# An LSTM layer on one core: the input projections of the first sixteen steps laid out anew, and the weight pieces for later steps formed in halves

## The reference

```python
xW = jnp.einsum('ntd,dk->tnk', x, Wx) + b

def step(carry, xw_t):
    prev_h, prev_c = carry
    a = xw_t + prev_h @ Wh
    i = jax.nn.sigmoid(a[:, :Hdim])
    f = jax.nn.sigmoid(a[:, Hdim:2 * Hdim])
    o = jax.nn.sigmoid(a[:, 2 * Hdim:3 * Hdim])
    g = jnp.tanh(a[:, 3 * Hdim:])
    next_c = f * prev_c + i * g
    next_h = o * jnp.tanh(next_c)
    return ((next_h, next_c), next_h)
_, hs = jax.lax.scan(step, (h0, c0), xW)
x = x + jnp.transpose(hs, (1, 0, 2))
```

## Time and profile before

| | us |
|---|---|
| median of 3 runs | 2538.99 |
| lowest to highest | 2538.72 to 2539.34 |
| the profiled execution, its own time | 2539.07 |
| its span, first to last instruction | 2537.3 |
| TensorE matmuls busy | 2518.5 (99%) |
| VectorE busy | 1983.7 (78%) |
| ScalarE busy | 1237.1 (49%) |
| mean granted TensorE clock | 0.999 |

### The profile page before, as it was taken

How to read it: one execution, slowest core, us unless ns; L and a number is a source line. 1 busy time by engine, 2 the same in 40 slices (tenths; PEclk the granted TensorE clock), 3 DMA queues, 4 the chain that set the end, 5 groups by cost and what they waited for, 6 DMA issues and landing times.

```text
span 2537.3 us, 157236 instructions
## 1 busy us (share of the span) xinstructions
PE 2518.5 (99%) x67166; PEld 1795.3 (71%) x67166; DVE 1983.7 (78%) x8532; ACT 1237.1 (49%) x5216; POOL 0.2 (0%) x4
## 2 busy tenths in 40 slices
PE   8999999999999999999999999999999999999998
PEld 3577777777777777777777777777777777777776
DVE  7877777777777777777777777777777777777776
ACT  5444444444444444444444444444444444444444
POOL 0000000000000000000000000000000000000000
PEclk9999999999999999999999999999999999999999
DMA  4101101011011010110110101101101011011000
GB/s 169 36 17 33 30 20 33 19 31 33 17 33 29 21 33 18 32 33 17 33 28 22 33 17 33 33 17 33 26 24 33 17 33 33 17 33 25 24 17 18
DMA packets 141017, 76.01 MB, mean 30 GB/s; under 512 B 8492, under 2 KB 139708, under 8 KB 140220
## 3 DMA queue, kind: packets, MB, share of 16 engines
q1 hardware_dynamic: 140548, 75.40, 11.3%
q10 hardware_dynamic: 440, 0.20, 0.0%
HBM read 42.02 MB, written 33.55 MB: 30 GB/s over the span
## 4 chain that ended last, share of the span: by engine, by line
PE 98%; DVE 1%; DMA 0%; ACT 0%; SPq 0%; issue 0%; DVEq 0%
PE odd L281 26%; PE even L287 25%; PE odd L287 25%; PE even L281 13%; PE s1t_sum L281 6%; PE plain_even L287 1%; PE plain_odd L287 1%; PE plain_odd L300 1%; PE plain_even L300 1%; DMA w_raw<-in_L_cond_Wx_dram 0%; DVE xw_lo L792 0%; DVE hw_lo L792 0%; DVE hT_hi L620 0%; DVE w_raw L789 0%; DVE f_c L671 0%
## 5 line engine op out<-in xcount | busy, mean ns | idle before, releaser
L671 DVE TENSOR_TENSOR f_c<-i_f,c_state 128x64 f32<-128x64 f32 x992 | 225.2, 227 | 438.0 <-ACT i_f L521 438.0
L521 ACT ACTIVATE i_f<-odd 128x128 f32<-128x128 f32 x496 | 142.9, 295 | 529.3 <-PE odd L287 529.3
L281 PE MATMUL odd<-xw_lo,xT_hi 128*32 128x256 f16 x7936 | 388.6, 273 | 0.0
L281 PE MATMUL odd<-xw_hi,xT_hi 128*32 128x256 f16 x7936 | 388.6, 273 | 0.0
L281 PE MATMUL odd<-xw_hi,xT_lo 128*32 128x256 f16 x7936 | 388.6, 273 | 0.0
L287 PE MATMUL odd<-hw_hi,hT_hi 128*32 128x512 f16 x3968 | 385.9, 379 | 1.2 <-DVE hT_hi L620 1.2
L287 PE MATMUL even<-hw_hi,hT_hi 128*32 128x512 f16 x3968 | 385.9, 379 | 0.3 <-DVE hT_hi L620 0.3
L287 PE MATMUL odd<-hw_lo,hT_hi 128*32 128x512 f16 x3968 | 385.9, 379 | 0.0
L287 PE MATMUL even<-hw_lo,hT_hi 128*32 128x512 f16 x3968 | 385.9, 379 | 0.0
L521 ACT ACTIVATE i_f<-even 128x128 f32<-128x128 f32 x496 | 142.9, 295 | 417.9 <-PE even L287 417.9
L537 ACT ACTIVATE tanh_c<-c_state 128x64 f32<-128x64 f32 x992 | 269.1, 271 | 97.8 <-DVE c_state L681 38.8
(11 more groups left out here) (113 smaller groups left out, 4141.4 us busy)
## 6 DMA issues: line engine op xcount, KB each, us to landing
x_ring<-in_x_dram SPq DMA_DIRECT2D x252, 128.0 KB, 2.8
out_dram<-x_ring SPq DMA_DIRECT2D x252, 128.0 KB
w_raw<-in_L_cond_Wx_dram SPq DMA_DIRECT2D x3, 1024.0 KB, 9.8
w_raw<-in_L_cond_Wh_dram SPq DMA_DIRECT2D x3, 1024.0 KB, 15.4
w_raw<-in_L_cond_Wx_dram SPq DMA_DIRECT2D x2, 512.0 KB, 4.8
w_raw<-in_L_cond_Wh_dram SPq DMA_DIRECT2D x2, 512.0 KB, 18.9
x_ring<-in_x_dram SPq DMA_DIRECT2D x6, 64.0 KB, 17.7
out_dram<-x_ring SPq DMA_DIRECT2D x5, 64.0 KB
```

The lines of the kernel that those rows point to most:

```text
L281: mm = nc.tensor.matmul(bank[j * N:(j + 1) * N, cols], x_part[:, pair, n, k * N:(k + 1) * N], w_part[:, n, k, j, :], start=False, stop=Fal ...
L521: nc.scalar.activation(i_f_half, bank_half, ACT.Sigmoid, scale=UNSCALE).then_inc(if_ready[two], 1)
L671: nc.vector.tensor_tensor(half_of(f_c[:, :], two), half_of(i_f[:, P:2 * P], two), half_of(c_state[:, :], two), ALU.mult)
```

## The change

The four banks `plain_even`, `plain_odd`, `even[1]` and `odd[1]` now serve the plain steps in turn. While the input weight tiles arrive, TensorE adds, after step 0's products of a tile, the hi x hi and hi x lo products of steps 1 to 3 of that tile, in place of `keep_going`; biases for steps 2 and 3 are spread after the first tile, and the lo x hi products follow for step 1 after the last input tile and for steps 2 and 3 after step 0. The 144 passes of steps 4 to 15 are dealt out over steps 1 to 13 by `passes_done`. `plain_recur` takes both products of hT_hi before that of hT_lo. Inputs of steps 1 to 3 are cast and split after the first tile. FORMED pieces are formed and split by halves of 128 x 512 with new steps for each half, casts and the bias difference have new steps, and ScalarE's seed of a pair's bank in steps 13 and 15 waits for o_gate. The `keep_going` bursts after the recurrent tiles stay.

```diff
-FORM_AT = (0, 1, 2, 3, 4, 5, 6, 6)
-CAST_AT = (3, 4, 5, 6, 7, 8, 9, 10)
-REST_AT = (7, 8, 9, 10, 11, 12, 13, 14)
-BIAS_AT = 7
+FORM_AT = ((1, 1), (2, 2), (3, 3), (4, 4), (5, 5), (6, 6), (7, 8), (8, 9))
+CAST_AT = (8, 9, 4, 5, 6, 7, 10, 11)
+REST_AT = ((12, 12), (13, 13), (6, 7), (9, 10), (10, 10), (11, 11), (14, 14), (14, 15))
+BIAS_AT = 0
+
+AHEAD = 4
+
+PASSES = 12
+
+
+def passes_done(step):
+
+    return min(34 * step // 3, PASSES * (PLAIN - AHEAD)) if step < 13 else PASSES * (PLAIN - AHEAD)
...
+        plain_banks = (plain_even, plain_odd, even[1], odd[1])
...
-            def plain(t):
-                if t == 1:
-                    pe.wait_ge(bias_ready, 1)
-                else:
-                    pe.wait_ge(plain_seeded, t - 1)
+            def spread_bias(*steps):
+
+                for t in steps:
+                    for j in range(J):
+                        mm = nc.tensor.matmul(plain_bank(t)[j * N:(j + 1) * N, :], spread[:, j * N:(j + 1) * N],
+                                              bias_rows[:, :], start=False, stop=False, skip_group_check=True)
+                return mm
+
+            def plain_hi(t, k):
+                for w in (xw_hi, xw_lo):
+                    plain_add(plain_bank(t), xp_hi, (0, 1), w, t, k)
+
+            def plain_lo(t):
                 pe.wait_ge(xp_ready, t + 1)
-                for part, w in ((xp_hi, xw_hi), (xp_hi, xw_lo), (xp_lo, xw_hi)):
-                    for k in range(J):
-                        plain_add(plain_bank(t), part, (0, 1), w, t % GROUP, k)
+                for k in range(J):
+                    plain_add(plain_bank(t), xp_lo, (0, 1), xw_hi, t, k)
+
+            def plain_passes(first, last):
+
+                for n in range(first, last):
+                    t, (part, k) = AHEAD + n // PASSES, divmod(n % PASSES, J)
+                    if n % PASSES == 0 or n == first:
+                        pe.wait_ge(plain_seeded, t + 1 - AHEAD)
+                        pe.wait_ge(xp_ready, t + 1)
+                    x_part, w_part = ((xp_hi, xw_hi), (xp_hi, xw_lo), (xp_lo, xw_hi))[part]
+                    plain_add(plain_bank(t), x_part, (0, 1), w_part, t % GROUP, k)
 
             def plain_recur(t):
                 pe.wait_ge(hT_hi_ready[0], t + 1)
                 if t == 1:
                     pe.wait_ge(hw_hi_ready, J * GATES)
-                for k in range(J):
-                    recur_add(plain_bank(t), hT_hi, hw_hi, k)
+                    pe.wait_ge(hw_lo_ready, J)
+                for w in (hw_hi, hw_lo):
+                    for k in range(J):
+                        recur_add(plain_bank(t), hT_hi, w, k)
                 pe.wait_ge(hT_lo_ready, t + 1)
                 for k in range(J):
-                    recur_add(plain_bank(t), hT_lo, hw_hi, k)
-                if t == 1:
-                    pe.wait_ge(hw_lo_ready, J)
-                for k in range(J):
-                    mm = recur_add(plain_bank(t), hT_hi, hw_lo, k)
+                    mm = recur_add(plain_bank(t), hT_lo, hw_hi, k)
                 mm.then_inc(gates_ready, 1)
...
-                    keep_going()
+                    if k == 0:
+                        spread_bias(2, 3)
+                        pe.wait_ge(bias_ready, 1)
+                        pe.wait_ge(xp_hi_ready, AHEAD)
+                    for t in range(1, AHEAD):
+                        plain_hi(t, k)
+                plain_lo(1)
                 pe.wait_ge(hT_lo_ready, 1)
...
-                if plain_steps > 1:
-                    plain(t + 1)
+                if plain_steps == PLAIN:
+                    for ahead in range(2, AHEAD):
+                        plain_lo(ahead)
+                elif plain_steps > 0:
+                    plain_passes(passes_done(t - 1), passes_done(t))
...
+            spread_bias(0, 1).then_inc(bias_spread, 1)
             for t in range(PLAIN):
                 step(t, t % BODY, BODY, t // BODY, PLAIN - t)
             pe.wait_ge(xw_lo_ready[P_A22], 2)
...
+                    else:
+                        act.wait_ge(o_ready, t + 1)
                     seed(r % 2)
...
-                if plain_steps > 2:
+                if plain_steps > AHEAD:
                     act.wait_ge(o_ready, t + 1)
-                    seed_plain(t + 2)
+                    seed_plain(t + AHEAD)
...
-                        act.wait_ge(w_diff_ready, piece + 1)
+                        act.wait_ge(w_diff_ready, 2 * piece + 2)
                         split_x_hi(n, *W_PLACE[n], k)
...
-                    if n == W_B11 and k < 2:
-                        cast_plain(k)
+                    if n == W_B11 and k == 0:
+                        cast_plain(0)
                 if k == 0:
                     act.wait_ge(bias_spread, 1)
                     nc.scalar.activation(bias_scaled[:, :], plain_odd[:, :], ACT.Copy).then_inc(bias_ready, 1)
-                if k == 2:
-                    cast_plain(2)
-                    cast_plain(3)
+                    for t in range(1, AHEAD):
+                        cast_plain(t)
...
                 for piece, (n, k) in enumerate(FORMED):
-                    if plain_steps > 0 and FORM_AT[piece] == t:
-                        form(n, k)
-                    if plain_steps > 0 and REST_AT[piece] == t:
-                        split_x_lo(n, *W_PLACE[n], k)
+                    for g in range(2):
+                        if plain_steps > 0 and FORM_AT[piece][g] == t:
+                            form(n, k, g)
+                        if plain_steps > 0 and REST_AT[piece][g] == t:
+                            split_x_lo(n, *W_PLACE[n], k, (g,))
...
-                v.then_inc(xw_lo_ready[n], 1)
+                if halves[-1]:
+                    v.then_inc(xw_lo_ready[n], 1)
```

More of the change, by code:

```diff
@@ L289, in recur_add, with plain_bank @@
                 return mm
-            def plain_bank(s):
-                return plain_odd if s % 2 else plain_even
+            def plain_bank(t):
+                return plain_banks[t % AHEAD]
             def plain_add(bank, part, halves, w, slot, k):
@@ L335, in first_step @@
             def first_step():
-                bank = plain_even
+                bank = plain_bank(0)
                 pe.wait_ge(xp_ready, 1)
@@ L475, in seed_plain @@
             def seed_plain(t):
-                nc.scalar.activation((plain_odd if t % 2 else plain_even)[:, :], bias_scaled[:, :],
+                nc.scalar.activation(plain_banks[t % AHEAD][:, :], bias_scaled[:, :],
                                      ACT.Copy).then_inc(plain_seeded, 1)
@@ L511, in step @@
                 if plain_steps > 0:
-                    bank = plain_odd if s % 2 else plain_even
+                    bank = plain_banks[t % AHEAD]
                     nc.scalar.activation(i_f[:, :], bank[:, IF], ACT.Sigmoid, scale=UNSCALE).then_inc(if_ready[0], 1)
@@ L733, in step @@
                 if plain_steps == PLAIN:
-                    rest_plain(2)
-                    rest_plain(3)
                     transpose_x(1, 1, 0)
@@ L775, in form_bias, with form @@
                                         ALU.subtract).then_inc(bias_diff_ready, 1)
-            def form(n, k):
+            def form(n, k, g):
                 k0, gates = W_PLACE[n]
-                place = raw(k0 + k, gates)
-                a, b, op, was, formed = {P_S3: (place, raw(k, 1), ALU.subtract, W_B22, 0),
-                                         P_S1: (place, raw(k, 0), ALU.subtract, W_B12, k + 1),
-                                         P_S2: (raw(2 + k, 1), place, ALU.add, W_B11, 2 + k + 1),
-                                         P_A22: (place, raw(k, 0), ALU.subtract, W_B21, 4 + k + 1)}[n]
+                place = raw(k0 + k, gates, g)
+                a, b, op, was, formed = {P_S3: (place, raw(k, 1, g), ALU.subtract, W_B22, 0),
+                                         P_S1: (place, raw(k, 0, g), ALU.subtract, W_B12, k + 1),
+                                         P_S2: (raw(2 + k, 1, g), place, ALU.add, W_B11, 2 + k + 1),
+                                         P_A22: (place, raw(k, 0, g), ALU.subtract, W_B21, 4 + k + 1)}[n]
                 dve.wait_ge(xw_hi_ready[was], k + 1)
@@ L787, in form @@
                 if formed:
-                    dve.wait_ge(w_diff_ready, formed)
+                    dve.wait_ge(w_diff_ready, 2 * formed)
                 nc.vector.tensor_tensor(place, a, b, op).then_inc(w_diff_ready, 1)
@@ L793, in split_lo, with split_x_lo @@
                                                       op0=ALU.mult, op1=ALU.subtract)
-            def split_x_lo(n, k0, gates, k):
+            def split_x_lo(n, k0, gates, k, halves=(0, 1)):
                 dve.wait_ge(xw_hi_ready[n], k + 1)
@@ L799, in split_x_lo @@
                 lo = xw_lo[:, n, k, :, :].rearrange("p j (g f) -> p g j f", g=2)
-                for g in range(2):
+                for g in halves:
                     v = split_lo(src[:, 2 * gates + g, :, :], hi[:, g, :, :], lo[:, g, :, :])
```

(14 more changed lines are left out.)

## The result

The changed kernel takes **2547.68 us** (median of 7 runs, 2546.13 to 2549.50) against 2538.86 for the kernel before, timed beside it (7 runs, 2538.72 to 2539.34): a ratio of 1.0033, 95% interval 1.0024 to 1.0043. It is 8.8 us slower where I forecast 1.9 slower. The profiled run took 2546.85, 7.78 more than the 2539.07 of the profiled run of before.

The account below looks back on a forecast made before the run. It took TensorE as the bound, with a 2.54 us chain limiting the changed steps; 2539.07 + 0.10 for step 16's later start + 1.70 for the clock's fall = 2540.9 us, range 2538.4 to 2542.0 for 8 in 10.

Parts of the forecast that it names:

- Steps 1 to 15: Input steps: eight of the first twelve last 5.13 us, four 5.18; their last recurrence ends 3.49 us early, at 106.70.
- The step of rows 5 and 6: From a recurrence's end to the next, a chain of 2.54 us against 2.59 of fill: removed work buys 0.05 a step.
- The stall: Before step 16, TensorE waits some 3.6 us for A22's last half on VectorE; step 16 begins 0.10 us later than before.
- The clock: Behind the stall before step 16, TensorE's clock falls to its lower level: +1.7 us (0 to 1.8), chance 0.50.
- Rival 1: Before step 16 the stall is there but the clock holds: 2539.2 us, chance 0.41.
- Step 0 ends as now: At the start, the added early work is hidden and wins nothing: step 1's recurrence starts at 32.09 as before.
- The sum: Whole run: the profiled 2539.07 plus 0.10 for step 16's start and 1.70 for the clock gives 2540.9 us.
- Rival 2: Before step 16, the A22 wait doesn't bind; step 16 starts at 109.5: 2536.0 us, chance 0.04.
- Rival 3: In step 0, the denser start is still granted half speed and ends 7.1 us late: 2546.3 us, chance 0.03.
- Rival 4: In the input steps, all 112 matmuls that leave count, at 54 ns each: 2532.5 us, chance 0.02.

Follow-up runs that it names:

- 3: Kernel before with only the half pieces at their new steps, TensorE's order kept: 2546.01 us, ratio 1.0027.
- 9: Changed kernel with pieces formed whole, one rest placed otherwise and 27 pad matmuls, so both programs have their old lengths; A22's wait not moved: 2541.57 us.
- 1: Changed kernel with TensorE's A22 wait moved from ahead of the loop to its first use in close_odd: 2540.85 us, ratio 1.0009.
- 7: 2 with pieces formed whole again, giving VectorE's program its old length: 2538.70 us.
- 2: Changed kernel with the half pieces formed, cast and split in the steps of before: 2541.10 us.
- 12: Kernel before with 101 small matmuls (202 instructions) more on TensorE before the loop: 2542.43 us, ratio 1.0014.
- 8: 2 with 27 small matmuls more on TensorE and pieces formed whole, both programs at their old lengths: 2536.08 us, ratio 0.9988 to the kernel before.
- 10: 9 with the A22 wait moved to close_odd and 26 pad matmuls: 2536.22 us.
- 11: Kernel before with 64 one-column memsets more on VectorE at its start: 2539.89 us.
- 6: 2 with 27 small matmuls more on TensorE at its start, giving its program the old length: 2538.25 us.
- 5: Kernel before with 16 one-column memsets more at VectorE's start: 2541.30 us, ratio 1.0009.

## Why the prediction was wrong, and where it was right

**Steps 1 to 15: right.** From step 1's recurrence to the end of step 15's I gave 74.61 us (8 x 5.13, 4 x 5.18, 10.26 and 2.59); measured 107.81 - 33.17 = 74.64. The starts of the recurrences lie 5.13 us apart in eight of the first twelve steps and 5.19 in four; a step of 5.13 holds 92 matmuls of 54 ns, 4.97, so the pauses of 0.15 before hT_hi are there. The step of rows 5 and 6, a chain of 2.54 against a fill of 2.38, was the right way to see that most of the removed matmuls buy nothing. ("From step 1 TensorE has no pause" passes over the 0.51 before 37.96, which the sum itself uses.)

**The stall: right, 0.2 short.** I gave 5.99 from the end of step 15's recurrence to step 16's; it is 6.20. The last half ends at 113.67 and TensorE starts 0.34 later, not 0.05: in 3 and 9 it starts 0.34 to 0.35 behind the half as well.

**The clock: right in kind, its size in part luck.** +1.7 forecast, 1.6 measured in after's profile, and it fell in after, 3 and 9, behind pauses of 3.4 to 3.7 us. But behind the same stall the fall cost 2.7 us in the profiles of 3 and 9, above the 0 to 1.8 that I allowed. Rival 1, the clock that holds, had 0.41; for a pause of this length that was too much. Behind the shorter pause of step 508 it fell in the profiles of 1 (2.22 us) and 7 (2.57) and not in those of after, 2 and 12 (1.93 to 2.08); by their spans it fell in four of ten runs of 1 and three of ten of 7.

**"Step 0 ends as now": off by 1.08** in this profile. In it tile 0 of the recurrent weights is cast at 20.26 and not at 18.40, behind its DMA, and VectorE's sixteen splits start at 21.00 and pause 0.33, against 20.40 and no pause. ScalarE's rows, before and after:

```profile
18.40 4.52 ACT L572 ACTIVATE hw_hi<-w_raw 128x512 f16<-128x512 f32 x8 [0.83 <-DMA w_raw<-in_L_cond_Wh_dram]
```

```profile
20.26 2.19 ACT L604 ACTIVATE hw_hi<-w_raw 128x512 f16<-128x512 f32 x4 [2.08 <-DMA w_raw<-in_L_cond_Wh_dram]
```

In the profiles of the other kernels with the new start step 1's recurrence starts at 32.78 (1), 32.05 (2), 31.87 (8), 31.57 (9) and 32.65 (10), and with the old one at 31.69 (3) to 33.09 (11). So the new start doesn't make it late as such; it moves by up to 1.6 us from one profile to the next. I read one row of a DMA's arrival as fixed.

**The sum: wrong by what wasn't in it.** Adding the terms to the profiled execution's 2539.07 took over two things as unchanged that were not: the 1.77 us outside the span and the tail behind the loop. The diff takes 54 instructions from TensorE's program and gives 16 to VectorE's. I costed them by the time they run and not by where they push the code behind them. That is the failed step: **+2.6 to 2.85** for the block behind the loop (7 less 8, 2 less 6, clock falls included; in after's profile, without a fall, it is 2.46) and **+2.3** outside the span (4.07 in 1 against 1.80 in 10). For a change that removes code the sum should have had this term, from nothing to some 2 us for each of the two places, and the page of before has the queues' rows that lead to it.

In terms of medians, against before: new order of work -3.2 to -2.9 (8 and 10); A22's wait and the clock +5.35 (9 less 10); the block behind the loop +2.6 to +2.85; the block behind the end +2.25. Together +7.0 to +7.6 of the 8.8 measured. **Some 1.2 to 1.8 us stay open**, about what experiments 1 and 2 missed by. Part may be late starts as in the profiled run. The larger part may be the clock: the fall behind A22's stall can cost 2.7 us instead of 1.6 (3, 9), and there can be one behind step 508's pause too, of which after's profile has none. The mean granted clocks point that way: 0.999 in the profiled run and one other, 0.998 in four runs, 0.997 in the slowest, where 0.001 of the span is 2.5 us of clock. It is not shown: after's spans scatter by 3.2 us (2542.1 to 2545.3), and only one run was profiled.

**Rival 2** (the wait doesn't bind, 2536.0) is what the kernel is worth once nothing stands in its way: 2536.22 in 10, 2536.08 in 8. **Rival 3**, the slow start at half clock, gave 2546.3, near the measured time by a cause that isn't there: no stretch before step 16 was granted less in a way that made step 0 late by 7 us. A time that fits is no proof of a mechanism. **Rival 4**, 2532.5, is refuted by 8 and 10: 3 us gained, not 6.5.

**The range** was 2538.4 to 2542.0 and left out 2547.68 by 5.7. Its width came from terms within the steps I had read; it had none for the stretch that I hadn't.

## What to carry to other kernels

When a piece of work is moved later, look for the wait that stands for it on the consuming engine and put it at the first use: here that one line is worth 5 us of 2540. Before judging a change of a few tenths of a per cent, compare the lengths of the engines' programs before and after, and look at the instruction queues: where a block of 256 instructions ended just behind the loop's end, a load of 2 to 2.5 us was exposed, and idle instructions ahead of the loop took it away. The 2.2 us behind the end also came and went with a few instructions, but which place in the program decides it wasn't found, so there the way is to look for a packet behind the last instruction. Experiment 10 with both repairs runs in 2536.22 us, 0.9988 [0.9979, 0.9998] of the kernel before.

## What the runs showed of the hardware

- In the seven kernels of the table the first code packet behind the loop came after the loop was left: the packet 0.5 to 1.2 us behind it, TensorE running on 2.4 to 2.7 us after that packet. TensorE stood for 1.9 to 2.6 us where the block was needed after 13 or 14 matmuls, and not at all where after 115.
- 16 instructions more in one engine's program cost 2.2 us behind the last instruction of the kernel (5); 64 more cost nothing there (11).
- The granted clock fell behind pauses of 3.4 to 3.7 us each time a profile showed one, and behind pauses of 1.9 to 2.6 us in two of five. A fall cost 1.6 to 1.7 us (after, and 1 behind step 508) or 2.7 (3 and 9) where matmuls cover everything.
- The fp32 bias spreads at the start took twice as long in after as in before (1.68 us from one bank to the next instead of 0.85) at a granted clock of 1.00, in 1, 2, 5 to 9 and 11 too, 5 and 11 with the old order among them, and not in 3 and 10. The cause is open; it is before the weights arrive and cost nothing that showed.
